# A new table for the order of all steps of a twelve-block perceiver kernel

## The reference

```python
x = x + _L0_xattn_ref(_layernorm(x, axis=-1), ctx_768, ...)
x = x + _L0_attn_ref(_layernorm(x, axis=-1), ...)
x = x + _L0_ffn_ref(_layernorm(x, axis=-1), ...)
...
x = x + _L3_xattn_ref(_layernorm(x, axis=-1), ctx_768, ...)
x = x + _L3_attn_ref(_layernorm(x, axis=-1), ...)
x = x + _L3_ffn_ref(_layernorm(x, axis=-1), ...)
```

```python
logits = xf @ gate_w.T
topk_logits, topk_idx = jax.lax.top_k(logits, TOP_K)
topk_w = jax.nn.softmax(topk_logits.astype(jnp.float32), axis=-1).astype(x.dtype)
comb = jnp.zeros((N, E), x.dtype).at[jnp.arange(N)[:, None], topk_idx].add(topk_w)
...
for e in range(E):
    y = jax.nn.silu(xf @ wg[e].T) * (xf @ wu[e].T) @ w_down[e].T
    out = out + comb[:, e:e + 1] * y
shared = jax.nn.silu(xf @ sg_gate.T) * (xf @ sg_up.T) @ sg_down.T
```

## Time and profile before

| | us |
|---|---|
| median of three runs | 2556.38 (2555.1 to 2557.56) |
| span of the profiled execution | 2557.4 |
| PE busy | 2254.9 |
| DVE busy | 1746.6 |
| ACT busy | 1368.6 |
| POOL busy | 774.0 |
| constant products L471, busy, of the 454 recorded | 131.0 |

### The profile page before, as it was taken

One profiled execution on the slowest core, in us unless ns is written; L12 is line 12 of the kernel. 1 busy time (PEld: TensorE's weight loads), 2 busy tenths in 40 slices (PEclk: granted clock), 3 DMA queues, 4 the chain that ended last, 5 costly groups with the idle time before them and its releaser, 6 DMA issues.

```text
span 2557.4 us, 62072 instructions
## 1 busy us (share of the span) xinstructions
PE 2254.9 (88%) x26420; PEld 1506.9 (59%) x26556; DVE 1746.6 (68%) x4832; ACT 1368.6 (54%) x2287; POOL 774.0 (30%) x676
## 2 busy tenths in 40 slices
...
DMA packets 50452, 84.14 MB, mean 33 GB/s; under 512 B 9536, under 2 KB 24768, under 8 KB 49792
## 3 DMA queue, kind: packets, MB, share of 16 engines
...
## 4 chain that ended last, share of the span: by engine, by line
PE 57%; DVE 25%; ACT 8%; issue 4%; POOL 3%; DMA 1%; SPq 1%; another core or an unknown queue 0%; DVEq 0%; POOLq 0%; ACTq 0%
PE psum L946 6%; PE psum L908 5%; PE psum L904 5%; PE psum L1606 3%; PE psum L463 2%; DVE c_L3x_most L1726 2%; PE psum L1699 2%; DVE c_L2x_mx L2081 2%; PE psum L1984 2%; DVE c_L2x_p L2087 1%; PE psum L471 1%; PE psum L1395 1%; PE psum L1976 1%; PE psum L773 1%; PE psum L778 1%
## 5 line engine op out<-in xcount | busy, mean ns | idle before, releaser
L893 POOL TENSOR_TENSOR c_L3f_h<-c_L3f_h,c_L3f_spread 128x512 f32<-128x512 f32 x96 | 121.3, 1283 | 188.8 <-DMA c_L3f_spread<-scratch 103.1
L471 PE MATMUL psum<-halves_held 128*128 128x512 bf16 x454 | 131.0, 403 | 14.0 <-issue 9.8
L936 DVE TENSOR_TENSOR c_L3f_h<-c_L3f_h,psum 128x512 f32<-128x512 f32 (+1 forms) x112 | 75.9, 682 | 76.5 <-PE psum L908 52.0
L922 ACT ACTIVATE c_L3f_h<-psum 128x512 f32<-128x512 f32 (+1 forms) x112 | 65.5, 594 | 110.2 <-PE psum L904 99.1
L946 PEld LDWEIGHTS psum<-weights,c_L3f_h 128*128 128x128 f32 (+1 forms) x896 | 108.1, 193 | 19.3 <-issue 15.3
L946 PE MATMUL psum<-weights,c_L3f_h 128*128 128x128 f32 (+1 forms) x896 | 112.9, 279 | 0.0
L904 PE MATMUL psum<-c_L3f_xT,weights 128*128 128x512 f32 x208 | 107.4, 601 | 0.0
L908 PE MATMUL psum<-c_L3f_xT,weights 128*128 128x512 f32 x208 | 107.4, 603 | 0.0
L471 PEld LDWEIGHTS psum<-halves_held 128*128 128x128 bf16 x588 | 54.3, 102 | 74.8 <-issue 35.1
L893 POOL TENSOR_TENSOR c_L0f_h<-c_L0f_h,c_L0f_spread 128x512 f32<-128x512 f32 x64 | 82.5, 1313 | 50.4 <-DVE c_L0f_h L936 39.2
L1606 PE MATMUL psum<-c_L3x_qx,c_L3x_kT 32*128 32x256 f32 x512 | 77.1, 427 | 21.1 <-DVE c_L3x_most L1726 17.4
...
## 6 DMA issues: line engine op xcount, KB each, us to landing
...
```

Of the source, the lines that this page charges most:

```text
L471: nc.tensor.matmul(j.psum[:, bank, :], j.half["ident"], j.half["take"], start=True, stop=True)
L893: nc.gpsimd.tensor_tensor(h, h, j.m["spread"][:, f, :], ALU.mult).then_inc(*j.up("mixed"))
L922: nc.scalar.activation(j.m["h"][P - rows:P, f, :], j.psum[0:rows, 1 + 2 * f % 3, 0:j.tok], ACT.Silu).then_inc(*j.up("silu"))
```

## The change

Only the string `ORDER` is another. Programs, buffers, jobs, `PLAN`, the count of steps of each engine and the nine `+` are the same. The counts of constant products sum to 525 in place of 588 and stand ahead of 158 steps in place of 198. Within their engine's own order, 829 of 2448 PE steps stand at another place (158 of them by three places or more), 2357 of 3306 on DVE (796), 769 of 1520 on ACT, 378 of 664 on POOL and 41 of 176 on SP.

```diff
--- before.py
+++ after.py
@@ -2838,76 +2838,76 @@
 ORDER = (
-    "vqQDDddDVdldkdddp8paglPLaDKQqDpDDLPaApgApGp7PvvdDavAkGKvvpPPP1paVVa3pgdAdaVpgdVlVPp1pA2PGvQvA4PDadvAkPGPlPvdvkV1pVa3pDDA"
-    "dLdvvDavvadavlVKpVvVPPAApGQPvvvA1PlvGvPvvdPDgkdVv9pVgAaVVVPpApGpapaDpaDLapDKQppvvpPaApDvavvaPavDkdpddDLA1PvlGpPvDvKvPvVV"
...
+    "dDqDddldkqQdddplVDaL2pDaKQDdDDPvpPagA1pgApLkpvGvD3PaAGvvVvpPaPKPg1paVAd5pagVdVdVPpAppvPlAlvda4PDAGQPGkvd5PvvD1PkVDpLVaAd"
+    "dDdvvlavdpavvaK1pVVvVP1PAApvvGkPvAlvG3PvQvvdPgPVvV9pgADDaDLaaVVaVPppppDapAppKDDDLDpQvvpPaAapaPaKpAPkdvvdvvdlGGvdldpvvPvP"
...
```

More of the change, by code:

```diff
@@ L2909 @@
[L2909 to L2910 removed]
+    "dDqDddldkqQdddplVDaL2pDaKQDdDDPvpPagA1pgApLkpvGvD3PaAGvvVvpPaPKPg1paVAd5pagVdVdVPpAppvPlAlvda4PDAGQPGkvd5PvvD1PkVDpLVaAd"
+    "dDdvvlavdpavvaK1pVVvVP1PAApvvGkPvAlvG3PvQvvdPgPVvV9pgADDaDLaaVVaVPppppDapAppKDDDLDpQvvpPaAapaPaKpAPkdvvdvvdlGGvdldpvvPvP"
+    "vVVAvvvgVVvVPAk6PApgDaPDApGpGQaPPkPVpVDpALaaaVDVVPppAppKvGDvpPaAvav1pvaPvDaDAdLdL1pGPvdDPlpvKvdPvVvVAvVvVvVVgPvA1pg+aVAV"
@@ new lines @@
+    "PVApVDApkPpapaaPpKDVVVVpaVDpVVpvVvGpaVD4pbGPLApLpDrrrPrrArPrrrADPrrrAPrrAPdrPrrKrrPrPaVvVPcAbpdaVAVPsAVpVApvdplKDPapaVpv"
+    "svPVgVspVagpsVpgVaVscgVDcGcVDcPvApgvpLPLDAPAPGPKPAAPPPVDVPAppaaPAcApAckPcKDDdDVLVgVVvvggLVcvPVpVaVDVpbVpVVpaGppVvPGdrApr"
+    "arrDPdrrrPrArrPArrArPdrrArPrvPrrKrPPaVVPcbpAvpasAPApAppaPpsapsPKDDVVDVLVlDvLvVgVgVpsVgpKVsagcVVcgDVdvcGcVcPGApagpPAPAPAP"
+    "APPkPPVVPAcvvgVAVPgVAcVAcvpadPpbppaPpappKDVrrrrrrvdrVrrVrVrrvrprarpvrarpVpvrrarpVpVVcvbDpGapVapvDPvdsAplpGPALPDdAPAPAPks"
@@ new lines @@
+    "PPgsKPgsVcgaVcsqgDcDPgvAdcgdcgPBgRdcRRlcddRRcRRRRPvRAPRRRPRpkRaPVRApRRapqvRVpRdddPCAldBadDapgPaVPSkvgAPvLvvPVAPVPdAgPdVP"
+    "vAPSvPVppGASpaaGPSaVGCDSCGpGCvGvCGCavlCvGKdCdCVPApavPDBDpRRaDRRPRLpRRkvpaPvpdRRRDadpdRRlpRRRARqaRRRapgRPaVCvBgPAvdvPVAPk"
+    "VPSdAgPvPpvpdadpaValPAVpPvvddS+PPaGvSGvCASGApavGPSVGkpaGPpvppaVdavpGapagAqpPaVCgvKCvGvdCCCgdCvlCvppaVdpad1PaddAklpPvvPaP"
+    "vPvBRdRpRavRRRApDRaRRRpRvpkdPdaDpdDdRRapRldARavpRaVqRgRRRpVCvaPBddgPkAvvPVAPSVPAgPvLPpvDpdapVaaPAVpPvSvPGSPavGCSvlCAASGp"
@@ new lines @@
+    "avGCVGdpaCGpvpkGvaPddpddapVapagqvGplCaCgKCvvdCdVPADdgPDBvRPRvPpRARdRaPVpRpRaRRaRRRkRARpRPvRvRPRRRPaVDCvBLPvld1pAavVSpkaP"
+    "ApVvppaddaddpapagSlpGdSqPadAvPgvPvGAvCSVdPSVCgdPvGPpvpapGaaPlAAGpGCvvDCVdaCvGkCvkpavPdpaCpvppadddapVvpKGaaqgpCaVPAgvlvPv"
+    "dBdRPdPAQgPvpvdpRaRpaldaDdDkVA1pPvvRPVPavPvApaAvRPDRRLRRpkRaRVpVRRRDvppaapRRRaRpvRKgaRDpvCaPBAgPvPvAVPSPAgv7pvpapadVaDDd"
+    "dplPvdSvPVGSPavGCSvkGCSGpavCGLpaG2pvGvCApddaCVDDpGpKvCvCvdCvVgDPAgppPvPvQvaAApGPAgvPvDppAVaVGVpVlVdDapaGpLVvvVvvp2PPAAPv"
```

123 lines of the change are left out of this document (55 added, 68 removed).

## The result

The changed kernel takes **2568.45 us** (median of 5, 2562.42 to 2573.36), the kernel before on the same chip 2555.12 us (median of 5, 2553.99 to 2557.56). The ratio is 1.0049, 95% interval [1.0035, 1.0064]: slower by some 13 us, where 17 us faster were forecast. The five executions had mean clocks of 0.964 to 0.971; the profiled one is the slowest of them (2573.36 us).

A forecast was written before the change was run, and what follows sets the result against it. No single bottleneck: PE, busy 2254.9 of 2557.4 us, loses time in many small order-dependent waits. Terms −2.7 − 3.5 − 2.7 − 8.4 = −17.3 us give 2540.1, as a median 2539 us; 8-in-10 range 2515 to 2562.

The forecast's parts named there:

- rival 3: Whole kernel: 63 products fewer leave PE longer pauses and a lower clock, a little beyond 2562 us; chance 0.10.
- my point of 0.961: Mean clock, in place of 0.971, from which clock loss outweighs the 17.3 us gain and makes the kernel 5.1 us slower.
- The price: Whole kernel: each us at the lower clock level costs 0.5 us on work filling 88% of the time, 0.44.
- Products, −3.5: Constant products at L471: 588 become 525, a quarter of 13.9 us lies on the chain; −3.5 us, bounds 0 to −13.9.
- Start, −2.7: 20 to 40 us: POOL roots move ahead of L612, so L604 starts near 34.8, not 37.56; −2.7 us, bounds 0 to −3.3.
- Late, −2.7: 2331 to 2342 us: POOL's root moves ahead of L893, shortening PE's wait for L384; −2.7 us, bounds +1.3 to −3.5.
- Early norms, −8.4: DVE, each job's first norm: chain pieces worth 16.8 us move behind other work; half counted, −8.4 us, bounds 0 to −16.8.
- my marker: DVE: pieces of early norms on the chain of waits fall from 33.8 us to about 17 to 25.
- the other 45 us of reversed links: DVE-to-DVE links on the chain reversed beyond the early norms' 16.8 of 61.8 us; no sum put on them.
- rival 2: Whole kernel: each removed wait is replaced by the other context's; only −4.5 us, median 2551.9; chance 0.18.
- The first sign: Whole kernel: the mechanism is wrong if PE's idle time falls by less than 10 us.
- Rival 4: Whole kernel: new meetings of DVE steps with POOL products lengthen steps and eat the gain, 2553 to 2561 us; chance 0.10.

The follow-up runs named there:

- e4: Kernel before in its old order, with the changed kernel's counts of constant products (525): 2578.73 us, 1.0074 against before.
- e3: Changed kernel's order with the old counts of constant products at each PE step (588): 2577.13 us, 1.0071 against before.
- e9: Kernel before in its old order, without any constant product: 2648.38 us, 1.036 against before.
- e2: Kernel before up to 2440 us, its remaining steps in the changed kernel's order: 2563.9 us, 1.0015 against before.
- e16: Kernel before with the new order and counts to 195 us only: 2557.95 us, 0.9988 against before.
- e15: Kernel before with the new order and counts from 2100 to 2409 us only: 2553.21 us, 0.9979 against before.
- e11: Kernel before with 196 more constant products in pauses of its own trace (784): 2559.63 us, 1.0015 against before.
- e10: Changed kernel with 209 more constant products in pauses of its own trace (734): 2575.27 us, 1.0068 against before.
- e6: Changed kernel's order with the larger of old and new product count at each place (736): 2577.01 us, 1.007 against before.
- e17: Changed kernel with only L2x's first context transfer (L533) issued ahead of weight load L3011 on SyncE: 2575.02 us, 1.0054 against before.

## Why the prediction was wrong

- **Which case came true.** The outcome is that of rival 3, slower by the clock, to which I gave 0.10. The mean clock of the changed kernel is 0.968, of before 0.973, and by the line this is 8.4 of the 9.4 us between their means. Its mechanism, fewer products, is only half of it: e4 loses clock by the counts alone, but e3, with all 588 products in the new order, stands at 0.968 too. It came true well short of my point of 0.961, because that point was set by 17.3 us of gains that had to be outweighed and of which almost nothing was there. The price was nearly right: mine is 2 × 2557 × 0.001 × 0.44 = 2.25 us per 0.001, the executions show 1.64. So the failure was in the size of the gains and in the chance more than in the price.
- **Why the chance was too small.** I argued that half of the removed products are in L2x and L2f, where 256 remain. What counts is where they stand. At 1200 to 1250 us fifteen went and the clock there is 0.90, beside 0.93 to 1.00 with them. My argument summed over whole stages what is decided place by place. That products hold the clock is shown by e9's 90 us, and that taking these 63 away costs time by e4; which of the exchanges in the middle cost what is not shown, but for the one at L1561.
- **Products, −3.5.** This is the step that failed, and e4 shows it: I priced the removed products by their share of the chain of waits alone and put what they do for the clock at nothing. In the old order their removal costs 19 us by the means in place of −3.5, by the line 11 of them clock. The bounds of the term, 0 and −13.9, did not even have its sign. The 25% was off as well, since it came from a trace with 134 products missing: e2's chain has 47.3 us of 588, a third, which would have made the term −4.6 and so more wrong. The chain of the changed kernel has 55.0 us of 525; I had said under 30. And the pitch of 0.243 us holds the first product's full time; in the changed kernel one product takes 0.38 us (at 30.31) and three take 0.81 (at 33.47), so a further one takes 0.215.
- **Start, −2.7.** Right: −2.55 at L604, and L571 at 30.66 (30 forecast). In the time, e16 gives 3 us by its ratio of 0.9988, and its interval holds 0: not shown there.
- **Late, −2.7.** The order did what I said (root first, L380 0.17), but the wait fell by 0.7 and not by 1.8, since L384 met five L893 in place of three: 4.95 us for 3.98. I had written that it would run beside L893 "in the same way". The lower clock behind the wait did go (the six L2615 behind it take 2.84 us in place of 3.48). The gain of the late part is real (e15, about 5 us), and most of it comes from 2200 to 2300 us, of which I had said that no order can give much since PE was 96.35% busy. It went to 99.85% and clock 1.00.
- **Early norms, −8.4.** The largest term, and no time shows any of it. The 240 pieces of before add up to 32.9 us when added again (I had 33.8); the changed kernel has 32.6, of which the blocked L417 is 9.5, so 23.1 without it. By that my marker (17 to 25) was met, and the time did not come with it. The marker is loose: before's order of DVE has 28.3 us in e4 and 27.1 in e11, the new one 29.3 in e3 and 19.2 in e10. No run moves these steps alone. But e3 is the new order with the old products, and it is 18 us slower by the means, 10 of them beside the clock. What the new order gained at some steps it lost at others, as at L1561, where I had put the other 45 us of reversed links at nothing. Time on the chain of waits is not time to be won when another flow is just as late, which I had written under rival 2 and not used here.
- **The sum.** By my own rule ("wrong in mechanism if PE's idle time falls by less than 10 us or the clock moves by 0.005") I was wrong on both counts. The idle time rose, and the mean clock of the executions fell by 0.005. The first sign was a poor one, though: by e4's trace, taking away 63 products turns some 23 us of busy time into idle time whatever the order does. Rival 4 is answered by DVE's busy time, to which only L417 adds.

What stays open: which exchanges of the middle cost the rest, and why the new order lowers the clock even with 588 products; which exchange brings the late gain; and whether L417 is blocked in every execution or only in some (it was in the profiles of the changed kernel, e2, e6 and e17 with 9.5 to 9.8 us, and not in e3 and e10, which have the same order there).
